# Gradient loop of a fused adaLN block: order of upstream products, Sigmoids and roundings

## The reference

```python
gate_before_act = w0 @ kT;  hidden_before_mul = w2 @ kT;  dhidden = w1.T @ vT
hidden = silu(gate_before_act) * hidden_before_mul
dhidden_before_mul = dhidden * silu(gate_before_act)
dgate_before_act = silu_backprop(dhidden * hidden_before_mul, gate_before_act)
dw1 = vT @ (hidden.T * lr1)
dw0 = dgate_before_act @ (k * lr0)
dw2 = dhidden_before_mul @ (k * lr2)
w_i = zeropower_ns5(dw_i)      # bf16(dw), divided by its Frobenius norm, 5 Newton-Schulz steps
w_i = w_i + dw_i               # then rows scaled back to the norms of the first weights, and applied to q
```

## Time and profile before

| what | us |
|---|---|
| median of 3 runs (682.58 to 685.45) | 683.43 |
| the profiled execution, its time | 680.91 |
| its span, from the first to the last instruction | 679.1 |
| TensorE busy in the span | 652.2 |
| DVE busy | 475.2 |
| ACT busy | 337.0 |
| GpSimd busy | 227.4 |

### The profile page before, as it was taken

One profiled execution on the slowest core, in us unless ns is written; L12 is line 12 of the kernel. 1 busy time (PEld: TensorE's weight loads), 2 busy tenths in 40 slices (PEclk: granted clock), 3 DMA queues, 4 the chain that ended last, 5 costly groups with the idle time before them and its releaser, 6 DMA issues.

```text
span 679.1 us, 11544 instructions
## 1 busy us (share of the span) xinstructions
PE 652.2 (96%) x4146; PEld 561.1 (83%) x4146; DVE 475.2 (70%) x925; ACT 337.0 (50%) x721; POOL 227.4 (33%) x221
## 2 busy tenths in 40 slices
PE   8999998799978999999999999999999999999997
PEld 7889898699966888888888888888888888888885
DVE  6988878899987787774457665566656565555545
ACT  3778699799976864532332222332222332222331
POOL 4578868858267641241003310123002330000000
PEclk7999999999999999999999999999999999999999
DMA  8000000150000000340023322243122342212132
GB/s 327 5 1 1 1 2 3 45 173 27 2 2 0 2 1 1 102 116 29 19 80 92 114 84 70 75 125 109 63 64 84 109 115 71 62 64 69 55 91 111
DMA packets 23095, 43.58 MB, mean 64 GB/s; under 512 B 3544, under 2 KB 5856, under 8 KB 22912
## 3 DMA queue, kind: packets, MB, share of 16 engines
q1 hardware_dynamic: 22624, 42.26, 19.8%
q10 hardware_dynamic: 416, 0.59, 0.3%
HBM read 40.60 MB, written 2.24 MB: 63 GB/s over the span
## 4 chain that ended last, share of the span: by engine, by line
PE 76%; DVE 10%; ACT 5%; POOL 5%; issue 2%; DMA 2%; DVEq 0%; SPq 0%; ACTq 0%; POOLq 0%
PE ps L1143 38%; PE ps L1220 19%; PE ps L949 3%; PE ps L1057 2%; PE ps L1068 2%; PE ps L1081 2%; PE ps L1082 2%; PE ps L990 2%; PE ps L1097 2%; PE ps L1186 1%; DVE x L1583 1%; ACT junk L712 1%; PE ps L1166 1%; POOL qk L433 1%; PE ps L918 1%
## 5 line engine op out<-in xcount | busy, mean ns | idle before, releaser
L842 ACT ACTIVATE sgm<-ps,zero 128x512 f32<-128x512 f32 x100 | 68.9, 690 | 273.0 <-PE ps L1143 273.0
L1143 PE MATMUL ps<-h2hi,whi 128*128 128x512 f32 x400 | 156.1, 390 | 0.0
L1143 PE MATMUL ps<-h2lo,whi 128*128 128x512 f32 x400 | 155.6, 389 | 0.0
L1143 PE MATMUL ps<-h2hi,wlo 128*128 128x512 f32 x400 | 155.6, 389 | 0.0
L1634 DVE TENSOR_TENSOR am<-sgm,ps 128x512 f32<-128x512 f32 x88 | 60.5, 688 | 135.6 <-ACT sgm L842 135.6
L523 POOL CAST whi<-raw 128x768 fp32r<-128x768 f32 x25 | 21.7, 866 | 242.0 <-DMA raw<-in_moew 242.0
L1143 PEld LDWEIGHTS ps<-h2lo,whi 128*128 128x128 f32 x400 | 75.1, 188 | 15.7
L1143 PEld LDWEIGHTS ps<-h2hi,whi 128*128 128x128 f32 x400 | 75.1, 188 | 15.5
L1143 PEld LDWEIGHTS ps<-h2hi,wlo 128*128 128x128 f32 x400 | 75.1, 188 | 15.3
L1643 DVE TENSOR_TENSOR pm<-am,cw 128x512 f32<-128x512 f32 x88 | 74.9, 851 | 5.2 <-DMA cw<-combine 2.8
L1220 PE MATMUL ps<-ahi,whi 128*128 128x512 f32 x200 | 77.9, 390 | 0.1
(11 more groups left out here) (212 smaller groups left out, 1187.0 us busy)
## 6 DMA issues: line engine op xcount, KB each, us to landing
raw<-in_moew SPq DMA_DIRECT2D x25, 384.0 KB, 3.9
cw<-combine SPq DMA_DIRECT2D x32, 256.0 KB, 3.2
cw<-combine SPq DMA_DIRECT2D x16, 224.0 KB, 2.9
cw<-combine SPq DMA_DIRECT2D x16, 192.0 KB, 2.8
cw<-combine SPq DMA_DIRECT2D x16, 160.0 KB, 2.7
wog<-combine SPq DMA_DIRECT2D x2, 1024.0 KB, 7.0
cw<-combine SPq DMA_DIRECT2D x16, 128.0 KB, 3.0
out<-x1T SPq DMA_DIRECT2D x8, 256.0 KB, 3.7
```

Of the source, the lines that this page charges most:

```text
L842: ac.activation(sgm[:, n % 2, :], gate_bank(n), ACT.Silu, bias=zero[:, :]).then_inc(S["e_sg"], 1)
L1143: last = mm(o, w_, a_[:, kc, tok], start=(kc == 0 and k == 0), stop=(kc == KC - 1 and k == 2))
```

## The change

TensorE issues the upstream products of batch b+1 ahead of the gradients of batch b-1, where before it was those of b. ACT's loop starts at batch 1; its Sigmoid is of batch b+1 and stands first, and the scaled values of b+1 stand last, behind the wait for the gradients of b-1. Batch 1's Sigmoid and scaled values stand ahead of the loop. On DVE the wait for the gradients of b-2 is moved from sg to hid, and the rounding is of batch b-2, between dhb and dgb, where it was of b-1 behind dgb; the rounding of batch 6 is behind the loop.

```diff
--- before.py
+++ after.py
@@ -686,6 +686,8 @@
             turned_q(NBLK - 1)
             ac.wait_ge(S["lr_ok"], 1)
             scaled_values(0)
+            sigmoid(1)
+            scaled_values(1)
 
             def sum_out(b):
                 ac.wait_ge(S["f_ps"], b + 1)
@@ -711,19 +713,18 @@
                         ac.wait_ge(S["f_ss"], m)
                     ac.activation(junk[:, :], X[:, m, :], ACT.Square, bias=zero[:, :], accum_out=fss[:, m:m + 1]).then_inc(S["f_ss"], 1)
 
-            for b in range(B):
-                if b >= 1:
-                    sigmoid(b)
-                if b >= 2:
-                    ac.wait_ge(S["dw_ps"], b - 1)
-                if b >= 1:
-                    scaled_values(b)
+            for b in range(1, B):
+                if b + 1 < B:
+                    sigmoid(b + 1)
                 if b >= 2:
                     grad_squares(b - 2, range(6) if b < B - 1 else range(3))
                 if b >= 1:
                     grads_out(b - 1)
                 if b >= 3:
                     sum_out(b - 3)
+                if b + 1 < B:
+                    ac.wait_ge(S["dw_ps"], b)
+                    scaled_values(b + 1)
             grad_squares(B - 3, range(3, 6))
             grad_squares(B - 2, range(0, 3))
             sum_out(B - 3)
@@ -1012,8 +1013,8 @@
 
             pe_.wait_ge(S["ident_ok"], 1 + NS_STEPS)
             for b in range(1, B + 1):
-                if b < B and b > 1:
-                    fast_up(b)
+                if b + 1 < B:
+                    fast_up(b + 1)
                 if b >= 3:
                     pe_.wait_ge(S["dw_sb"], NH * (b - 1))
                     if b >= 4:
@@ -1326,8 +1327,6 @@
 
                 i = b % 2
                 ve.wait_ge(S["sig"], b + 1)
-                if b >= 2:
-                    ve.wait_ge(S["dw_ps"], b - 1)
                 if b >= 1:
                     ve.wait_ge(S["b_dg"], b)
                 ve.tensor_tensor(sg[:, :, :], s_sb[i][:, :, :], gate_ps(i), ALU.mult).then_inc(S["b_sg"], 1)
@@ -1337,6 +1336,8 @@
             def gate_products(b):
 
                 i = b % 2
+                if b >= 2:
+                    ve.wait_ge(S["dw_ps"], b - 1)
                 ve.tensor_tensor(hid[i][:, :, :], sg[:, :, :], hid_ps(i), ALU.mult).then_inc(S["b_hid"], 1)
                 ve.tensor_tensor(dhb[i][:, :, :], sg[:, :, :], dh_ps(i), ALU.mult).then_inc(S["b_dhb"], 1)
 
@@ -1395,12 +1396,13 @@
                 if b >= 1:
                     gate_slopes(b)
                     gate_products(b)
+                if b >= 2:
+                    cast_grads(b - 2)
                 ve.wait_ge(S["b_ds"], b + 1)
                 ve.tensor_tensor(dgb[i][:, :, :], u[:, :, :], hid_ps(i), ALU.mult).then_inc(S["b_t"], 1)
                 ve.wait_ge(S["b_t"], b + 1)
                 ve.tensor_tensor(dgb[i][:, :, :], dgb[i][:, :, :], dh_ps(i), ALU.mult).then_inc(S["b_dg"], 1)
-                if b >= 1:
-                    cast_grads(b - 1)
+            cast_grads(B - 2)
             for b in range(3):
                 x_init(b)
             first_turned(1)
```

## The result

The changed kernel takes 686.12 us, the median of 20 runs (683.91 to 688.15), against 684.54 for 20 runs of the kernel before on the same chips (681.04 to 688.00). The ratio is 1.0032, with a 95% interval of 1.0020 to 1.0044: slower by 2.2 us, between 1.4 and 3.0. The forecast was slower by 1.8.

A forecast was written before the change was run, and what follows sets the result against it. TensorE's 5.55 a batch sets the loop's pace, ACT as full at 5.61; Br lands +0.5 without contention, +1.8 with it, so 683.43 + 1.8 = 685.2, range 681.6 to 687.2.

The forecast's parts named there:

- (1) U ahead of G: TensorE's queue: upstream products U(b+1) go ahead of gradients G(b-1); G(0) 2.6 later, work unchanged, only idle time can go.
- (2) The key products as the link: GpSimd's key products, waiting for G(b-2), become the link to dgb: 11.2 for two batches against TensorE's 11.1; Br +0.5.
- Rival B: ACT's fixed order decides and gains and losses cancel, or products not truly further ahead: 0, 683.4; chance 0.10.
- rival A: No meeting of GpSimd and DVE, or meetings off the path: +0.5, 683.9; chance 0.22.
- (3) Contention: GpSimd's key products meet DVE's u in nearly every batch, 0.40 and 0.35 longer; G(7) +1.4, Br +1.8.
- rival D: GpSimd's chain sets the pace from batch 2 on, with whole blocking and roundings beside the slope: +3.5, 686.9; chance 0.10.
- The end of the loop: TensorE idles about 2 ahead of G(6), again ahead of G(7), on ACT; G(7) at 115.7, another 0.4 lost behind it.
- The clock: TensorE's granted clock at its upper level, 2.4 GHz; idle 1.59 and 1.79 in the loop did not lower it: counted nothing.

The follow-up runs named there:

- the run with the 5 products: Changed kernel with 5 extra products of ones by ones, result unused, in TensorE's idle time ahead of G(6): 685.39, ratio 1.0009.
- the third buffers: Changed kernel with a third buffer for each of GpSimd's two key products, which then wait for the gradients of b-3: 685.17, ratio 1.0002.
- the run with half of the squares: Changed kernel with ACT's squares of the odd matrices of batches 0 to 6 left out (norms differ from the reference): 686.34, ratio 1.0035.
- the run with third buffers and half of the squares: Changed kernel with third buffers for the key products and ACT's squares of odd matrices of batches 0 to 6 left out: 681.63, ratio 0.9959.
- DVE's part: Kernel before with only DVE's edits: rounding of b-2 between dhb and dgb, wait for gradients of b-2 on hid: 696.58, ratio 1.0173.
- the order alone: Changed kernel with DVE's edits taken back, so only TensorE's and ACT's order is changed: 686.99, ratio 1.0037.
- old order: Two runs of the kernel before: with third buffers for the key products, 685.77, ratio 1.0013; with half of ACT's squares left out, 683.44, ratio 0.9986.

## Why the prediction held

**Direction and size.** Forecast 685.2 in a range of 681.6 to 687.2, with 0.88 on less than half a per cent: measured 686.12, or +2.2 by the ratio against the forecast +1.8. The agreement of the sizes is in part luck. The +1.8 was laid out as the delay of Br, and Br came later than that: from a start at 74.85 at 126.0 without a fall of the clock (the run with the 5 products), +3.2, and at 128.2 with one, +5.3, where the text had 124.6.

**(1) U ahead of G.** As forecast: U(2) took the place of G(0), G(0) came 2.7 later, and of TensorE's idle time none was saved. From a start at 74.85 the G stood at 77.6, 82.9, 89.2, 94.8, 101.0, 106.5, 112.3 and 118.9, where the text had 77.6, 83.1, 89.0, 94.6, 100.5, 106.1, 111.0 and 115.7. The first six are within 0.5.

**(2) The key products as the link.** Right, and shown: the third buffers take the waits of U away and bring G(6) 2.2 forward, in the new order and not in the old; the run with half of the squares shows that ACT's load does not hold the loop up to G(5). Rival B, under which ACT decides, is out for that part. (For rival A the text gives GpSimd slack in four of seven batches; it waits for u in five.)

**(3) Contention.** Right in kind, and the first term that was mis-sized. The key products took 2.8 in batches 2 to 5, as laid out from the rows, and u 1.02 in batches 3 and 4. But the roundings, costed at 0.5 and given 0.16 more only in rival D, took 0.92, 1.01, 0.92 and 1.58 in batches 2 to 5. The first and third started beside the last key product, the other two beside the slope, and each ended 0.4 behind the end of the GpSimd instruction that it met (84.16 behind 83.74, 90.70 behind 90.28, 102.69 behind 102.28). The slopes of batches 2 and 4, which came second, took 1.58 instead of 1.28. The nearest row had a rounding beside the key products at 0.72. The Trainium skill, SBUF — State Buffer, section "Who interferes with whom", says this of a DVE cast in a two-port mode against GpSimd: whoever starts second is blocked whole. The trace agrees for the roundings, and by that rule they would have belonged in the forecast. G(6) came 1.3 later than laid out; 0.5 of that is seen on the path, as ACT's squares of batch 3 waited 0.52 for the rounding of 1.58, and the rest is not divided. That moving the roundings back to their old place gained nothing (1.0037) shows that they were not alone on the path: there sg waits for the rounding instead.

**The end of the loop.** Right in kind: TensorE waits 2.41 ahead of G(6) (about 2 forecast) and again ahead of G(7), for ACT's copy and sum. Two terms were mis-sized. G(7) came at 116.8 without a fall, 1.1 later than laid out, at the end of the chain that the text names: there the norms of batches 0 and 1 took 3.4 on GpSimd (102.23 to 105.62) instead of 2.9, and the other links a little more each. And from G(7) to Br it took 9.2, where the text had 8.9 and the kernel before 8.5. With half of the squares G(6) came 1.4 earlier and G(7) only 0.4: it hangs on that chain, and not on G(6). The run with third buffers and half of the squares shows what is left of these when ACT is light, 1.08 and 1.16: the way from the last result of G through copy and sum. U(7) used to cover it between G(5) and G(6).

**The clock.** This step had no ground: "did not lower it, so I count nothing for it". It argued from idle times of 1.59 and 1.79 in one execution that idle time does not matter, and did not ask what the 2 us it had itself laid out ahead of G(6) would do. In the profiled execution G(6) took 2.6 longer at the lower clock, and the loop 2.1 longer than in the run with the 5 products. That nothing is yet near the truth in the medians is luck too: the kernel before has as many runs with a low clock (20 of 29 under 0.990, against 7 of 20), so what the falls cost stands on both sides.

**What stays open.** In its loop the changed kernel without a fall is 3.2 behind the kernel before (51.2 against 48.0), while the ratio of that run is 1.0009, +0.6, at most +1.9. The profiled execution of the kernel before took 680.91, under the lowest of its 20 runs in the same comparison, and shows no fall between 20 and 670 us, so it is likely not a typical one; the run with the 5 products is 6.1 above it, 3.2 of it in the loop, and has the four falls shown above. Profiles of more executions of each kernel would tell how often a fall meets the loop, and what the loop of the kernel before takes as a rule. What starts a fall is open as well.

## What to carry to other kernels

Issuing a producer earlier moves time only if all that its consumer waits for comes earlier: here every path to dgb still went through a GpSimd step released by the gradients of two batches back, and slack on that engine (8.7 us of waiting for u) turned into waits on DVE (5.7) and TensorE (0.69 and 0.47). Before such a change, follow each buffer's release as well as each operand, lay out the last iterations by themselves, where a cover such as U(7) is gone, and take idle time of TensorE that the layout creates as a risk for the work behind it. One profile without a fall of the clock does not show that there is none. Parts of a change in order can be bad alone (+12 us for DVE's part) and harmless together, so look for the cycles that they form across the queues, and test the parts together as well as one by one.

## What was not expected of the hardware

- TensorE's granted clock fell to 0.5 inside stages that are otherwise full, and the length of the idle time ahead does not tell where. It fell behind 2.41 (changed kernel), 2.09 (third buffers), 1.75 (the order alone, in the midst of G(6)), 1.94 and 2.03 (old order), 2.68 (half of the squares), 2.04 and 3.13 (DVE's part alone). It did not fall behind 2.61, 2.00 and 2.01 in that last run, behind 1.79 in the profiled execution of before, nor behind the 1.76 ahead of G(7) in the run with 5 products. In that run it fell at 68.5, where TensorE was busy from 61 on. A block G took 5.3 instead of 2.7 at the lower clock. In the three profiles with filler products in an idle time the stretch behind them was at 1.00.
- A rounding of 128x768 to bf16, 0.55 alone, took up to 1.58 beside a GpSimd product of two SBUF tiles of 128x512, and ended 0.4 behind it; that product, 1.28 alone, took 1.58 where the rounding had started first.
